# Macaron block on one core: another order for the middle weights, and three router marks on ScalarE

## The reference

```python
x = x + 0.5 * ffn(layernorm(x))      # the first experts
x = x + attn(layernorm(x))           # the middle: linear attention and a gelu MLP
x = x + 0.5 * ffn(layernorm(x))      # the second experts
```

```python
oh = one_hot(routes); pos = (cumsum(oh, 0) * oh).sum(-1) - 1
keep = pos < capacity
slot = where(keep, routes * capacity + pos, E * capacity)
buf = zeros.at[slot].set(x)          # 8 experts x 256 rows
out = where(keep, y_flat[slot], x)
```

## Time and profile before

| | |
|---|---|
| median of 3 runs | 689.31 us (688.82 to 691.78) |
| the profiled execution, its own time | 691.69 us |
| its span | 689.9 us |
| TensorE matmul busy | 649.3 us (94%) |
| VectorE, ScalarE, GpSimd busy | 519.2, 467.9, 368.7 us |
| mean granted TensorE clock | 0.98 of full speed |
| TensorE's share of the chain that ended last | 54% |

### The profile page before, as it was taken

How to read it: one execution, slowest core, us unless ns; L and a number is a source line. 1 busy time by engine, 2 the same in 40 slices (tenths; PEclk the granted TensorE clock), 3 DMA queues, 4 the chain that set the end, 5 groups by cost and what they waited for, 6 DMA issues and landing times.

```text
span 689.9 us, 18063 instructions
## 1 busy us (share of the span) xinstructions
PE 649.3 (94%) x6437; PEld 571.9 (83%) x6437; DVE 519.2 (75%) x1346; ACT 467.9 (68%) x933; POOL 368.7 (53%) x540
## 2 busy tenths in 40 slices
PE   7789998998789999999999999999999996999997
PEld 5559998975678898888888888888888774899997
DVE  7868898825678777868878778778767458789882
ACT  5688887704457786777767677676754654898882
POOL 5254565755766545455584774855735655244312
PEclk9879999999999999999999999999999998999999
DMA  8399879425766554544565455554451535677750
GB/s 261 120 297 317 283 218 334 148 68 109 111 105 105 96 97 71 105 85 70 116 91 113 86 91 128 71 110 89 62 100 35 177 95 113 185 231 225 237 158 31
DMA packets 284803, 95.66 MB, mean 139 GB/s; under 512 B 213988, under 2 KB 281664, under 8 KB 284714
## 3 DMA queue, kind: packets, MB, share of 16 engines
q1 hardware_dynamic: 267610, 82.30, 49.1%
q0 software_dynamic: 4992, 11.49, 5.5%
q10 hardware_dynamic: 12112, 0.72, 1.1%
HBM read 65.10 MB, written 29.44 MB: 137 GB/s over the span
## 4 chain that ended last, share of the span: by engine, by line
PE 54%; DVE 7%; POOL 4%; issue 4%; ACT 3%; ACTq 1%; DMA 1%; SPq 1%; POOLq 0%; DVEq 0%
PE bank L2098 49%; PE bank L2107 5%; POOL hids L1002 2%; ACTq L476 1%; DVE den L1916 1%; DVE att_ L1914 1%; DVE kv_ L1941 1%; POOL sth L987 1%; DVE hn_ L1961 1%; DMA keys<-qkv_rows 1%; DMA xb_rows<-late_rows,xb_token 0%; DVE ots L1907 0%; SPq L476 0%; ACT L1333 0%; ACTq L482 0%
## 5 line engine op out<-in xcount | busy, mean ns | idle before, releaser
L2098 PE MATMUL bank<-hnts,up_w 128*128 128x512 f32 (+1 forms) x432 | 106.0, 382 | 0.1
L2098 PE MATMUL bank<-down_w,hids 128*128 128x256 f32 x768 | 104.5, 284 | 1.2 <-POOL hids L1002 0.6
L1002 POOL TENSOR_TENSOR hids<-hid,hids 128x512 fp32r<-128x512 f32 (+1 forms) x67 | 82.0, 1225 | 36.2 <-ACT hids L1309 36.2
L2098 PEld LDWEIGHTS bank<-down_w,hids 128*128 128x128 f32 x768 | 96.5, 188 | 4.2 <-POOL hids L1002 2.0
L2098 PEld LDWEIGHTS bank<-hnts,up_w 128*128 128x128 f32 x432 | 71.2, 189 | 10.3 <-ACT hids L1309 0.3
L2098 PE MATMUL bank<-qkv_w,xnts 128*128 128x256 f32 (+1 forms) x384 | 76.9, 348 | 1.6 <-DVE xnts L1927 0.9
L2098 PEld LDWEIGHTS bank<-qkv_w,xnts 128*128 128x128 f32 x384 | 60.5, 189 | 18.6 <-issue 5.7
L1304 ACT ACTIVATE hid<-bank,cols 128x512 f32<-128x512 f32 (+1 forms) x72 | 45.7, 640 | 39.5 <-PE bank L2098 39.2
L968 POOL TENSOR_SCALAR stz<-stz 128x1 f32<-128x1 f32 x32 | 7.2, 226 | 113.9 <-DVE stz L1945 113.9
L2098 PE MATMUL bank<-xa_xt,a_w 128*128 128x256 f32 x384 | 52.1, 286 | 2.9 <-ACT xa_h L1143 2.0
L2098 PE MATMUL bank<-xb_xt,b_w 128*128 128x256 f32 x384 | 51.6, 284 | 0.1
(11 more groups left out here) (307 smaller groups left out, 1641.4 us busy)
## 6 DMA issues: line engine op xcount, KB each, us to landing
qkv_rows<-feats SPq DMA_DIRECT2D x32, 384.0 KB, 2.7
a_raw<-in_L_ffn_w_dram SPq DMA_DIRECT2D x32, 256.0 KB, 4.1
a_w<-in_L_ffn_w_dram SPq DMA_DIRECT2D x32, 256.0 KB, 4.4
b_raw<-in_L_ffn_w_dram SPq DMA_DIRECT2D x32, 256.0 KB, 3.3
b_w<-in_L_ffn_w_dram SPq DMA_DIRECT2D x32, 256.0 KB, 3.0
mid_rows<-x_all SPq DMA_DIRECT2D x8, 512.0 KB, 4.2
values<-qkv_rows SPq DMA_DIRECT2D x32, 128.0 KB, 3.0
late_rows<-x_ SPq DMA_DIRECT2D x8, 512.0 KB, 3.1
```

Source lines behind the costliest of these rows:

```text
L1002: pool.tensor_tensor(hids[1][u % 3][:, 0:w], hid[u % 2][:, 0:w], f32(hids[0][u % 3][:, 0:w]), ALU.subtract).then_inc(s_hidl, 1)
L2098: return pe.matmul(dst, left, right, start=start, stop=stop, skip_group_check=True)
```

## The change

Five edits, in three functions of the router and in the tables of the first experts:

1. The chunks of the middle's weights go by a table of units, `CHUNK_UNITS`: 10, 11, 12, 14 to 18 and 20 to 27, so nothing at 13 and 19. The first chunk of `fc_w` moves from unit 18 to unit 20, the last from 25 to 27.
2. SyncE loads `fc_w` at unit 15 ahead of that unit's expert weights instead of behind them, and `proj_w` at unit 20 instead of 17. `fc_w` now waits for the low part that VectorE makes at unit 16 (the sixth chunk), before at unit 15. The reload of q, k and v at unit 28 waits for `fc_w` to have landed, no longer for its last chunk.
3. The marks of tiles 13, 14 and 15 are made by ScalarE: `Abs(position - place)`, then `Relu(1 - that)`, six instructions, behind the last copy of logits and ahead of expert 0's weights.
4. TensorE sums the marks of tiles 0 to 12, runs 3 idle products, sums tiles 13 to 15, runs 2 more, and then counts batch 1.
5. `xa_token` is made from the sums at once, as max(number - 1, 0); `empty_a` and `slot_a` are made behind it. An empty slot now fetches token 0 instead of the last token.

```diff
-        LATE = 10
+        PIECES_FROM = 6
+        CHUNK_UNITS = (10, 11, 12, 14, 15, 16, 17, 18) + tuple(range(20, 28))
+        MARKS_BY_ACT = range(BATCH - 3, BATCH)
...
             for u in range(E * PAIRS):
                 x, j = divmod(u, PAIRS)
+                if u == CHUNK_UNITS[SHIFTED] - 2:
+                    load_piece(2)
                 if x + 2 < E:
                     load_weights(x + 2, xa, j)
...
-                elif LATE <= u < LATE + len(chunks):
-                    i = chunks[u - LATE][0]
-                    if i + 2 < len(pieces) and chunks[u - LATE + 1][0] != i:
-                        load_piece(i + 2)
+                if u == CHUNK_UNITS[chunks_through(1)]:
+                    load_piece(3)
                 if u == (E - 1) * PAIRS:
                     sp.wait_ge(xa.sem.low1, lows_made(E - 1, PAIRS - 1, False))
-                    sp.wait_ge(s_wlow, chunks_through(2))
+                    sp.wait_ge(*piece_loaded(2))
...
+            def marks_a():
+                act.wait_ge(s_adisp, placed(0))
+                for n in MARKS_BY_ACT:
+                    act.activation(mark_a[n][:], place[:], ACT.Abs, bias=small_a[:, 2, n:n + 1],
+                                   scale=-1.0).then_inc(s_axt, 1)
+                for i, n in enumerate(MARKS_BY_ACT):
+                    act.wait_ge(s_axt, NT + i + 1)
+                    act.activation(mark_a[n][:], mark_a[n][:], ACT.Relu, bias=first_wins[:, 0, E - 1:E],
+                                   scale=-1.0).then_inc(s_axt, 1)
...
                 if ex.slots is None:
-                    dve.wait_ge(s_atab, 3)
-                    dve.tensor_scalar(ex.buf.token[:], ex.buf.slot[:, :, 0], T - 1, None, ALU.min).then_inc(ex.sem.token, 1)
+                    dve.wait_ge(s_atab, 1)
+                    dve.tensor_scalar(ex.buf.token[:], number_a[:], -1.0, 0.0, ALU.add, ALU.max).then_inc(ex.sem.token, 1)
+                    slots_a()
...
                 for n in range(b * BATCH, (b + 1) * BATCH):
+                    if n in MARKS_BY_ACT:
+                        continue
...
-            number_slots_a(0)
+            number_slots_a(0, range(MARKS_BY_ACT.start))
+            idle_products(3)
+            number_slots_a(0, MARKS_BY_ACT)
+            idle_products(2)
             count_a(1)
-            number_slots_a(1)
+            number_slots_a(1, range(BATCH, NT))
```

More of the change, by code:

```diff
@@ L672, in _ @@
                     store_quad(NG - 1)
[L673 removed]
+                if u == PIECES_FROM:
                     sp.wait_ge(s_atab, 4)
@@ L1203, in _ @@
                     soften_a(0)
+            marks_a()
             for c in range(PAIRS):
@@ L1215, in middle_weights @@
                     pass_rows(NG // 2 + ST + u // 2, range(u % 2 * 2, u % 2 * 2 + 2))
-                if LATE <= u < LATE + chunks_through(2):
-                    i, k, c = chunks[u - LATE]
-                    if u < LATE + SHIFTED:
-                        act.wait_ge(s_shifted, u - LATE + 1)
+                at_u = chunk_at(u)
+                if at_u is not None:
+                    i, k, c = chunks[at_u]
+                    if at_u < SHIFTED:
+                        act.wait_ge(s_shifted, at_u + 1)
                     else:
@@ L1678, in finish, with slots_a @@
                                              op1=ALU.add).then_inc(ex.sem.fin, 1)
+            def slots_a():
+                dve.tensor_scalar(empty_a[:], number_a[:], 0.0, float(NOWHERE + 1), ALU.is_equal, ALU.mult).then_inc(s_atab, 1)
+                dve.wait_ge(s_atab, 2)
+                dve.scalar_tensor_tensor(out=slot_a, in0=number_a[:], scalar=-1.0, in1=empty_a[:], op0=ALU.add,
+                                         op1=ALU.add).then_inc(s_atab, 1)
             def run_experts(ex, between=None, meanwhile=None):
                 if ex.slots is None:
-                    dve.wait_ge(s_atab, 3)
-                    dve.tensor_scalar(ex.buf.token[:], ex.buf.slot[:, :, 0], T - 1, None, ALU.min).then_inc(ex.sem.token, 1)
+                    dve.wait_ge(s_atab, 1)
+                    dve.tensor_scalar(ex.buf.token[:], number_a[:], -1.0, 0.0, ALU.add, ALU.max).then_inc(ex.sem.token, 1)
+                    slots_a()
                     dve.wait_ge(s_bias_raw, 16 * 7)
@@ L1846, in _ @@
             dve.tensor_reduce(number_a[:], number_sums.rearrange("p (c f) -> p c f", f=2), AX, ALU.add).then_inc(s_atab, 1)
-            dve.wait_ge(s_atab, 1)
-            dve.tensor_scalar(empty_a[:], number_a[:], 0.0, float(NOWHERE + 1), ALU.is_equal, ALU.mult).then_inc(s_atab, 1)
-            dve.wait_ge(s_atab, 2)
-            dve.scalar_tensor_tensor(out=slot_a, in0=number_a[:], scalar=-1.0, in1=empty_a[:], op0=ALU.add,
-                                     op1=ALU.add).then_inc(s_atab, 1)
             def middle_weights(u):
-                if LATE <= u < LATE + chunks_through(2):
-                    i, k, c = chunks[u - LATE]
+                at_u = chunk_at(u)
+                if at_u is not None:
+                    i, k, c = chunks[at_u]
                     view, (high, low) = piece_view(i), pieces[i][0]
-                    dve.wait_ge(s_whigh, u - LATE + 1)
+                    dve.wait_ge(s_whigh, at_u + 1)
                     high, low = (piece_cut(i, w, k, c, False) for w in (high, low))
@@ L1864, in middle_weights @@
                         dve.tensor_tensor(low, piece_cut(i, view, k, c, True), f32(high), ALU.subtract).then_inc(s_wlow, 1)
-                if 0 <= u - LATE + 1 < SHIFTED:
-                    i, k, c = chunks[u - LATE + 1]
-                    if u == LATE - 1:
+                at_u = chunk_at(u + 1)
+                if at_u is not None and at_u < SHIFTED:
+                    i, k, c = chunks[at_u]
+                    if at_u == 0:
                         dve.wait_ge(s_mean, 3)
@@ L2323, in count_a, with number_slots_a @@
                 mm(dst, ones_bf[:], seen_a[:, b:b + 1].broadcast_to([P, BATCH, E]), stop=True).then_inc(s_acount, 1)
-            def number_slots_a(b):
+            def number_slots_a(b, rows):
                 sums = number_sums.rearrange("p (e s f) -> p s e f", s=ST, f=2)
                 pe.wait_ge(s_apick, 8 * (b + 1))
-                for n in range(b * BATCH, (b + 1) * BATCH):
-                    pe.wait_ge(s_amark, n + 1)
+                for n in rows:
+                    if n in MARKS_BY_ACT:
+                        pe.wait_ge(s_axt, NT + len(MARKS_BY_ACT) + n - MARKS_BY_ACT.start + 1)
+                    else:
+                        pe.wait_ge(s_amark, n + 1 - b * len(MARKS_BY_ACT))
                     for s in range(ST):
```

5 lines of the change are left out of this document (3 added, 2 removed).

## The result

| | before | the change | ratio, 95% interval |
|---|---|---|---|
| first measurement | 690.21 us | 695.51 us | 1.0057 [1.0042, 1.0072] |
| second | 691.18 us | 693.58 us | 1.0037 [1.0014, 1.0059] |
| third | 690.88 us | 693.28 us | 1.0035 [1.0019, 1.0051] |

The change makes the kernel slower by 0.35 to 0.57%, 2.4 to 3.9 us; forecast were 3.2 us faster. The profiled execution of the first measurement was disturbed (a span of 2168.5 us), so the profile after is that of the second: 693.23 us, span 691.5, mean granted clock 0.981.

A forecast was written before the change was run, and what follows sets the result against it. TensorE, busy 94% of the span, was taken as the bound, so savings count only where it waits. 2.4 (loads) + 0.61 (marks) + 0.15 (tokens) = 3.2 us; 689.31 - 3.2 = 686.1 us, range 684.9 to 688.9.

The forecast's parts named there:

- Part 1, where `fc_w` goes out: Experts, unit 16: VectorE's low part done at 99.95, so SyncE issues `fc_w` at about 100.0, against 99.75 before.
- the 0.42 that one chunk less was to save: VectorE before unit 16's low part: one chunk less ahead of it makes it 0.42 us earlier.
- Part 1, what stands behind it: Expert 5's last quarter, behind `fc_w`: `a_raw` out at 100.5, landing at 107.5, ScalarE waiting some 2 us, TensorE losing nothing.
- a landing up to 109.9 costs TensorE nothing: Unit 19: `a_raw` landing by 109.9 still lets unit 20's relus finish before TensorE wants them at 111.4.
- The cover of two units: Units 19 to 21: ScalarE's wait for `a_raw` moves one unit back, where there are 3.07 us more of room.
- Part 1, the gain of 2.4 us: Experts from 100 to 120 us: TensorE's gaps of 2.00 and 0.31 us and perhaps 0.1 of small ones go.
- Parts 2 and 3: Router: three marks fewer on VectorE gain 0.61 us; tokens from the sums start the gather 0.42 sooner, 0.15 counting.
- the sum of 0.61 and 0.15: Router: the gain from three marks fewer plus the counted part of the earlier gather, some 0.8 us at the first `up`.
- the bound of 0.50: Router: each of ScalarE's six mark instructions priced at 0.50 us, after the nearest measured instruction.
- the cover held: Router: ScalarE's work behind the marks ends at about 30.5, rescaling starts at 31.1, leaving 0.6 us of cover.
- Slower: Rival, unit 16: VectorE's low part about 2 us late delays `fc_w` and `a_raw`; about 2.5 us slower, 691.8; chance 0.06.
- The wait changes its place: Rival: expert 5's last quarter lands 11.8 us after issue, TensorE waits 2.3 us, Part 1 gives nothing; 688.5; chance 0.15.

The follow-up runs named there:

- ahead_early: later_reads with the load of `fc_w` ahead of unit 15's expert weights, its wait ending with the sixth low part at unit 15; ratio to before 0.9975.
- later_reads: Before with only `fc_w` read from unit 20 and `proj_w` loaded at unit 20; chunks 0 to 7 and the load of `fc_w` as before; ratio 0.9975.
- behind: Before with the change's table of units and `proj_w` at unit 20, but `fc_w` loaded behind unit 15's expert weights; no router part; ratio 0.9966.
- marks_alone: Before with only the three marks made by ScalarE, without the five idle products; ratio 0.9994.
- tokens: Before with only the tokens made from the sums, an empty slot fetching token 0; ratio 1.0007.
- marks: Before with only the three marks by ScalarE and the five idle products; ratio 1.0028.
- idle_alone: Before with only the five idle products, VectorE making all 16 marks; ratio 1.0037.
- idle_again: Second profile and measurement of idle_alone, before with only the five idle products; ratio 1.0036.
- router_no_idle: Before's table and loads, with three marks by ScalarE and tokens from the sums, without idle products; ratio to before 0.9988.
- whole_behind: The whole change, but with `fc_w` loaded behind unit 15's expert weights as before; ratio to before 0.9988.
- whole_no_idle: The whole change without its five idle products; ratio to before 1.0045.
- table: Before with only the change's table of units and moved loads of `fc_w` and `proj_w`; ratio 1.0011, measured again 1.0045.

## Why the prediction was wrong

**Part 1, where `fc_w` goes out: the step that failed.** The prediction says: "done at 99.95. The load is issued at about 100.0". The low part was done at 103.11 and `fc_w` went out at 103.14. Of the 3.16 us by which the low part was later, 0.90 came from a later start of the experts in this profile and 1.52 from the instruction that met GpSimd's; the rest, 0.74, is the 0.42 that one chunk less was to save, which was not there, and 0.3 more. Unit 16 now makes the sixth chunk, and other than the seventh it is shifted first, ahead of its low part (0.48 us at 98.32); the prediction took the time of the seventh. The 0.90 is by chance; the 1.52 comes with the table: in all nine profiles with nothing at units 13 and 19 the instruction at about 100 us takes 2.19 to 2.21 us, in all ten with chunks 0 to 7 at units 10 to 17 it takes 0.68 or 0.69, and there `xa_hs`, behind the low part, takes 2.01 or 2.02. The trace of before had this price in it; the prediction took each VectorE instruction at its time alone and did not ask on which side of the awaited low part the meeting would fall.

**Part 1, what stands behind it.** That "a landing up to 109.9 costs TensorE nothing" was the right kind of bound, for the wrong load. `a_raw` took 5.6 us, less than the 7 taken, and landed at 109.15; but ScalarE's quarter waits for `b_row` as well, which went out behind it and landed at 110.86. The code says so, and the prediction did not price it. And expert 6's loads went out in one burst behind the same wait: the `a_raw` of 107.95 landed only at 117.05, and ScalarE waited for it too. TensorE's largest gap, 1.65 us at 121.58, comes behind that one, so the second turn lost more than the first (14.46 and 13.38 us). The cover of two units was counted to one reader, and the queue behind it was not followed.

The four loads landed at 108.04, 109.15, 110.86 and 111.9, in the order of their issue. The rule of the Trainium skill (DMA: Bandwidth & Descriptors, Queues, rings and completion order) is that each DMA engine consumes one issuer's ring in order; the trace agrees with it. `fc_w` itself took 4.9 us there, not 9.2, so being behind it was cheap; ahead_early shows the same.

**Part 1, the gain of 2.4 us** was real where the last quarter was not held back: later_reads has 1.7 and behind 2.4. That `fc_w` is read two units later, with `proj_w` loaded later, brings it; the two were not run apart. The size came from the gap of one profile, 2.00 us; by the averages of the groups it is 2.2.

**Parts 2 and 3** held as far as the tokens: from the first choice to them it is 16.01 us before and 15.00 in the change, 1.01 less, for 0.61 + 0.42. From the first choice to the first `up` it is 26.5 to 27.7 us in six profiles with before's router (27.17 on average) and 26.38, 26.42 and 26.42 in the three with the router of the change: 0.76 us, as the sum of 0.61 and 0.15 said. With a spread of 1.2 us over six profiles of one router, that it fits so closely is luck, and marks_alone (27.36) and tokens (27.55), with one part each, show no gain there: the rows landed 4.3 us behind the start of the gather in both, 3.9 in before. ScalarE's six instructions were cheaper than the bound of 0.50, and the rescaling still waited 1.42 us, so the cover held. Idle products were priced at nothing; in the change they cost about 0.45 us of that distance (25.96 on average in five profiles without them), and far more in marks, idle_alone and idle_again. But 0.76 us is 0.11%, and no ratio shows it: router_no_idle, at 0.9988, fits it and fits no change as well. whole_behind has the later reads too, and should then be near 0.996; its 0.9988 is some 2 us above that, at the edge of what the intervals allow, and why is open.

**The rivals.** "Slower" was the mechanism that came: the low part late, `fc_w` and `a_raw` out at 102 and 102.5 (measured 103.14 and 103.55), 2.5 us slower (measured 2.4 to 3.9). It had been given 0.06. It was written as an accident that needs a lateness of 1 us together with a slow landing (11.8 us). The lateness came with the table; expert 5's quarter landed in 5.6 to 7.3 us and was late all the same, because SyncE had stood so long, and only the loads behind it took 9 us. In whole_no_idle a lateness of 0.95 us by the clock of the span, 1.7 from the turn of rows, was enough. "The wait changes its place" described the wait of 4.32 us rightly, and stopped one step short of its price.

## What to carry to other kernels

A load moved ahead in an in-order queue brings its wait with it: price the wait at the time when the engine it waits for is really done, and follow everything behind it, down to the smallest load that the same reader needs. If the purpose is that a reader should not wait, moving the reader later was worth 1.7 us by itself here (later_reads), and moving the load ahead took 3.2 us away in one pair of kernels and 4.8 in another. Where two engines slow each other, look which instruction the meeting hits after the change: one that an engine waits for, or one behind it. And test a table without the queue's new place before the two are joined.

## What the runs showed of the hardware

- A VectorE instruction with two inputs, 128 x 512, takes 0.68 us alone and 2.01 to 2.21 where GpSimd's product of 1.29 to 1.32 us begins beside it: the sum of the two or 0.2 more. It was so in all 19 profiles, with one instruction or another. The Trainium skill (GPSIMD Engine Reference, 1. Specifications) says that GpSimd's way to the memory on the chip is shared with VectorE, with contention for VectorE instructions with two inputs from there; the trace agrees.
- Five idle products on TensorE at 26 to 28 us, alone, cost 2.5 us of 690 in two measurements. In the three profiles of marks, idle_alone and idle_again the gathered rows landed 1.0 to 2.4 us later than elsewhere. The link between the two is not known.
- Three gaps of TensorE of 2.08 to 2.22 us were followed by a stretch at 1.2 GHz (granted clock 0.57 to 0.62 over 4 us), others of 2.00 and 2.65 were not (1.00).
- Executions of before spread by 4.8 to 6.5 us within a set, and a kernel's two measurements, on different chips, differed by up to 0.34% (table). Parts of 0.1% can be told in the trace, by distances between marks, but not by the time.
